# Conditioning every block in fp32 with row tiles of the array, in place of an fp16 high/low split

## The reference

```python
# x (128, 64, 512) fp32, itok (128,) in 1..198, weights (200, 64, 64), W1 (2048, 512), W2 (512, 2048)
w = weights[conditions]
c = jnp.einsum('bct,bcd->bdt', x, w)                 # conditioning, one 64x64 matrix per batch
h = gelu(einsum('bsd,hd->bsh', c, ternarize(W1)) + b1)
y = einsum('bsd,hd->bsh', h, ternarize(W2)) + b2
scale = jnp.max(jnp.abs(y)) / 7 + 1e-8               # over the whole tensor
out = x + jnp.clip(jnp.round(y / scale), -7, 7) * scale
```

## Time and profile before

| | |
|---|---|
| median of 3 runs | 1046.1 us |
| the profiled execution | 1043.87 us |
| its span, first to last instruction | 1042.1 us |
| mean granted TensorE clock | 0.966 of full |
| TensorE busy | 938.8 us (90%) |
| VectorE, ScalarE, GpSimd busy | 648.3, 553.5, 157.8 us |
| HBM read, written | 60.89, 16.78 MB |

### The profile page before, as it was taken

The page is one execution under the profiler, slowest core; times in us unless marked ns, Lnnn a source line. Parts: engine busy times, 40 slices in busy tenths (PEclk is TensorE's granted clock), DMA queues, the critical chain, the costliest instruction groups (busy, mean ns, idle before and its releaser), DMA issues.

```text
span 1042.1 us, 15005 instructions
## 1 busy us (share of the span) xinstructions
PE 938.8 (90%) x5265; PEld 449.3 (43%) x5265; DVE 648.3 (62%) x1005; ACT 553.5 (53%) x708; POOL 157.8 (15%) x213
## 2 busy tenths in 40 slices
PE   0599999999999999999999999999999999999600
PEld 0355444444444444444444444444444444444200
DVE  3499766666665657666666666566666656633492
ACT  3389282736446473828274564738282645536290
POOL 4022303030110303030301102030303021000000
PEclk9799999999999999999999999999999999999855
DMA  6610030211121211203011112112030111104899
GB/s 219 201 44 4 18 74 12 63 26 42 44 47 40 50 40 36 54 10 73 17 40 45 45 40 50 40 45 46 10 79 11 40 46 44 40 0 173 297 395 384
DMA packets 40560, 77.89 MB, mean 75 GB/s; under 512 B 3920, under 2 KB 4320, under 8 KB 40032
## 3 DMA queue, kind: packets, MB, share of 16 engines
q1 hardware_dynamic: 36272, 73.47, 24.1%
q0 software_dynamic: 4096, 3.94, 1.3%
q10 hardware_dynamic: 176, 0.27, 0.1%
HBM read 60.89 MB, written 16.78 MB: 75 GB/s over the span
## 4 chain that ended last, share of the span: by engine, by line
PE 77%; issue 10%; ACT 4%; DVE 3%; POOL 2%; DMA 1%; DVEq 0%; ACTq 0%; SPq 0%; POOLq 0%
PE ps L430 38%; PE ps L442 35%; PE ps L418 3%; ACT y L667 2%; PE ps L460 1%; ACT y L639 1%; POOL ws L342 1%; DVE st L684 1%; DMA yx<-in_x 1%; DVE y L797 0%; DVE y L932 0%; DVE wts L794 0%; DMA condb<-in_itok_B 0%; DVE st L743 0%; POOL wg L342 0%
## 5 line engine op out<-in xcount | busy, mean ns | idle before, releaser
L430 PE MATMUL ps<-yc,wts 128*128 128x512 f16 x2048 | 447.3, 379 | 0.2 <-ACT g L571 0.2
L442 PE MATMUL ps<-wts 128*128 128x512 f16 x1920 | 419.3, 379 | 0.7 <-ACT wts L595 0.7
L430 PEld LDWEIGHTS ps<-yc,wts 128*128 128x128 f16 x2048 | 199.5, 98 | 238.5 <-ACT g L571 0.7
L442 PEld LDWEIGHTS ps<-wts 128*128 128x128 f16 x1920 | 185.8, 98 | 220.4 <-ACT wts L595 0.9
L717 DVE SCALAR_TENSOR_TENSOR wts<-g,st,wts 128x512 f16<-128x512 f32 x256 | 186.4, 749 | 144.4 <-ACT wts L576 142.5
L571 ACT ACTIVATE g<-ps,b1t,st 128x512 f32<-128x512 f32 x256 | 197.9, 773 | 117.8 <-PE ps L430 107.2
L576 ACT ACTIVATE wts<-g,st 128x512 f16<-128x512 f32 x256 | 181.0, 713 | 0.0
L558 ACT ACTIVATE xs<-yx,st 128x2048 f16<-128x2048 f32 x28 | 56.1, 2002 | 143.5 <-DVE st L752 143.5
L364 POOL PARTITION_ALL_REDUCE st<-st x46 | 21.5, 468 | 670.2 <-DVE st L686 414.7
L342 POOL DMA_INDIRECT wg<-in_L_cond_weights,ids x112 | 106.5, 951 | 41.3 <-issue 29.6
L722 DVE SCALAR_TENSOR_TENSOR y<-ps,st,b2b 128x512 f32 (+1 forms) x56 | 41.8, 747 | 78.1 <-PE ps L442 78.0
(11 more groups left out here) (118 smaller groups left out, 379.4 us busy)
## 6 DMA issues: line engine op xcount, KB each, us to landing
yx<-in_x SPq DMA_DIRECT2D x56, 512.0 KB, 6.1
wts<-in_x SPq DMA_DIRECT2D x5, 1024.0 KB, 5.5
y<-in_x SPq DMA_DIRECT2D x5, 1024.0 KB, 10.4
out<-wts SPq DMA_DIRECT2D x10, 512.0 KB, 10.6
y<-in_L_ffn_W SPq DMA_DIRECT2D x8, 512.0 KB, 8.8
y<-in_L_ffn_W SPq DMA_DIRECT2D x4, 1024.0 KB, 8.3
wts<-in_x SPq DMA_DIRECT2D x8, 512.0 KB, 7.3
out<-y SPq DMA_DIRECT2D x4, 1024.0 KB, 12.6
```

What stands on the lines that cost most here:

```text
L430: last = nc.tensor.matmul(psH[:, j % HB, :], T1T[:, k, j * P:(j + 1) * P], csp[:, a, k, :], start=(k == 0 and a == 0), stop=(k == KT - 1 a ...
L442: last = nc.tensor.matmul(psY[:, r % 2, :], hsp[:, a, j, r * P:(r + 1) * P], T2T[:, j, :], start=(j == 0 and a == 0), stop=(j == HT - 1 an ...
```

## The change

All 16 blocks are conditioned in fp32 by one code. `xd` becomes a buffer of its own, loaded once for a block by four transfers: partitions 0 to 63 (s = 0) hold two batches of each half (h), partitions 64 to 127 (s = 1) the other two. `wg` shrinks to four matrices side by side in each side's 64 partitions, gathered by four indirect DMAs with 128 indices. Each matmul takes 64 partitions, either side alone, and writes that side's bank of `psC`. The splitting of x and w, its scales, its reductions and its semaphores are gone on VectorE, ScalarE and GpSimd, and so is `cinv` in the copy of c. `idt`, a temporary of the index arithmetic, moves to a part of y, and block 0's x of the tail goes to `xd`.

```diff
 # SP
-            load_direct(0)
-            sp.wait_ge(w_gathered[1], 16 * HALF)
+            def load_x(first_batch):
+                for s in range(2):
+                    for h in range(2):
+                        sp.dma_start(xd[s * C:(s + 1) * C, 2 * h:2 * h + 2, :],
+                                     x_cbt[:, bass.ds(first_batch + HALF * h + 2 * s, 2), :]).then_inc(xd_loaded, 16)
+            load_x(0)
+            sp.wait_ge(w_gathered, 16 * RT)
             for n in range(RT):
                 sp.dma_start(w2s[:, n, :], W2_v[:, n, :]).then_inc(w2_loaded[n], 16)
-            load_half(0, DIRECT * BB)
-            sp.wait_ge(t1_made, WCH)
-            sp.wait_ge(w1abs_made, LOADS)
-            load_direct(1)
-            with sp.Fori(1, 2 * (NB - DIRECT)) as n:
-                sp.wait_ge(x_split, n)
-                load_half(n, n * HALF + DIRECT * BB)
+            with sp.Fori(1, NB) as b:
+                sp.wait_ge(c_made, 2 * b)
+                load_x(b * BB)
 # GpSimd
-            def gather(b, columns, direct=False):
-                nc.gpsimd.tensor_copy(ids[:, :], columns).then_inc(ids_made, 1)
-                pool.wait_ge(ids_made, b + 1)
+            def gather(b, columns):
+                by_side = columns.rearrange("p (h s j) -> p s h j", h=2, s=2)
+                for s in range(2):
+                    side = slice(s * C, (s + 1) * C)
+                    nc.gpsimd.tensor_copy(ids[side, :].rearrange("p (h j) -> p h j", h=2), by_side[side, s, :, :])\
+                        .then_inc(ids_made, 1)
+                pool.wait_ge(ids_made, 2 * b + 2)
                 pool.sem_inc(pool_waited, 1)
-                for j in range(BB):
+                for r in range(RT):
...
             all_max(max2_part, 1, mx2r, mx2, max2_all)
+            pool.wait_ge(max2_all, 1)
             pool.wait_ge(c_made, 2)
-            gather(1, idx[:, BB:2 * BB], direct=True)
+            gather(1, idx[:, BB:2 * BB])
...
                 all_max_c(i + 1)
+                pool.wait_ge(cmax_all, i + 2)
                 gather(i + 2, columns)
-                for h in range(2):
-                    all_max(xw_part, 2 * i + 1 + h, xwr, xw, xw_all)
 # TensorE
+            def condition(b, half):
+                pe.wait_ge(xd_loaded, 64 * b + 64)
+                pe.wait_ge(w_gathered, 16 * RT * (b + 1))
+                pe.wait_ge(c_copied, 2 * b + half)
+                tiles(half, psC)
+            def tiles(half, bank):
                 for k in range(KT):
-                    tk = slice(k * P, (k + 1) * P)
-                    if direct:
...
-                    for j in range(HALF):
-                        n = half * HALF + j
-                        for a in range(2):
-                            last = nc.tensor.matmul(psC[:, k, j * C:(j + 1) * C], xs[:, n, tk], ws[:, a, n, :],
-                                                    start=(a == 0), stop=(a == 1))
+                    for j in range(2):
+                        for s in range(2):
+                            side = slice(s * C, (s + 1) * C)
+                            last = nc.tensor.matmul(bank[:, s, k, j * C:(j + 1) * C],
+                                                    xd[side, 2 * half + j, k * P:(k + 1) * P], wg[side, 2 * half + j, :],
+                                                    start=True, stop=True)
                 last.then_inc(c_made, 1)
 # ScalarE: high_x is gone from block_step and hidden; copy_c copies without a scale
 # VectorE, block_step
                 max_y(i, 1, tile_y(1), slot(1))
-                if not last_block:
-                    max_xw(2 * i, 0, i + 2)
                 store_y(i, 2, tile_y(2))
                 max_y(i, 2, tile_y(2), slot(2))
-                if not last_block:
-                    scale_xw(2 * i, 0, lk)
-                    low_x(2 * i, 0)
...
                 for j in range(HT):
                     low_h(i + 1, j)
-                    if j == 1:
-                        max_xw(2 * i + 1, 1, i + 2)
-                    if j == 3:
-                        scale_xw(2 * i + 1, 1, lk)
-                    if j == 6:
-                        low_x(2 * i + 1, 1)
```

More of the change, by code:

```diff
@@ L157, in build @@
         parts = rest.rearrange("p (w m n t) -> p w m n t", w=3, m=4, n=2)
-        xtail = [place(xs[:, :, :].rearrange("p b t -> p (b t)").bitcast(FP32)),
+        xtail = [place(xd[:, :, :].rearrange("p r t -> p (r t)")),
                  t1_rows[:, 0, :, :, :], t1_rows[:, 1, :, :, :],
@@ L183, in build @@
         sum2, sum2r = stat(2), stat(2)
-        xw, xwr, bxw, pxw, rxw, sxw = (stat(2) for _ in range(6))
-        cinv = stat(2)
         n2c, alpha2 = stat(), stat()
@@ L333, in _ @@
             link(nc.gpsimd.tensor_tensor(idx[:, :], idx[:, :], idt, ALU.add))
-            def gather(b, columns, direct=False):
-                nc.gpsimd.tensor_copy(ids[:, :], columns).then_inc(ids_made, 1)
-                pool.wait_ge(ids_made, b + 1)
+            def gather(b, columns):
[5 more added lines that the diff above has]
+                pool.wait_ge(ids_made, 2 * b + 2)
                 pool.sem_inc(pool_waited, 1)
-                for j in range(BB):
-                    side = slice(j % 2 * C, (j % 2 + 1) * C)
+                for r in range(RT):
                     nc.gpsimd.indirect_dma_start(
[L343 to L348, removed]
+                        out=wg[:, r, :], out_offset=None, in_=w_rows[:, :],
+                        in_offset=bass.IndirectOffsetOnAxis(ap=ids[:, r:r + 1], axis=0)).then_inc(w_gathered, 16)
+            gather(0, idx[:, 0:BB])
             nc.gpsimd.memset(ident[:, :], 0.0)
@@ L476, in _ @@
             nc.tensor.transpose(psY[:, 0, 0:HT], b1r[:, :], idf[:, :]).then_inc(b1_turned, 1)
-            condition(0, 0, direct=True)
-            condition(0, 1, direct=True)
+            pe.wait_ge(xd_loaded, 64)
+            pe.wait_ge(w_gathered, 16 * RT)
+            tiles(0, psC)
+            tiles(1, psC0)
             pe.wait_ge(b1_ready, 1)
@@ L545, in _, with copy_c @@
             act.dma_start(b2b[:, :], b2.rearrange("(a n) -> a n", a=1).to_broadcast([P, T])).then_inc(b2_loaded, 16)
-            def copy_c(b, half, direct=False):
+            def copy_c(b, half, bank=psC):
                 act.wait_ge(c_made, 2 * b + half + 1)
                 rows = slice(half * HALF * C, (half + 1) * HALF * C)
[L550 to L557, removed]
-                nc.scalar.activation(xs[:, js, :], xd, ACT.Copy, scale=sxw[:, 0:1])
-                nc.scalar.activation(ws[:, 0, js, :], wg[:, js, :], ACT.Copy, scale=sxw[:, 1:2]).then_inc(xhi_made, 1)
+                nc.scalar.activation(cf[:, :, rows].rearrange("p k (s r) -> p s k r", s=2), bank, ACT.Copy).then_inc(c_copied, 1)
             def high_c(b):
@@ L613, in _ @@
             relu1(1)
-            copy_c(0, 0, direct=True)
-            copy_c(0, 1, direct=True)
+            copy_c(0, 0)
+            copy_c(0, 1, psC0)
             relu1(2)
@@ L640, in _, with block_step @@
                     .then_inc(w2_counted, 1)
-            def block_step(i, first_block=False, last=False):
+            def block_step(i, first_block=False):
                 if not first_block:
@@ L646, in block_step @@
                     copy_c(i + 1, 0)
-                copy_c(i + 1, 1, direct=first_block)
+                copy_c(i + 1, 1)
                 high_c(i + 1)
-                if not last:
-                    high_x(2 * i, 0)
-                hidden(i + 1, lambda j: high_x(2 * i + 1, 1) if j == 5 and not last else None)
+                hidden(i + 1, lambda j: None)
             block_step(0, first_block=True)
-            with act.Fori(1, NB - 2) as i:
+            with act.Fori(1, NB - 1) as i:
                 block_step(i)
-            block_step(NB - 2, last=True)
             act.wait_ge(y_stored, RT * (NB - 1))
```

89 lines of the change are left out of this document (14 added, 75 removed).

## The result

| | before | after |
|---|---|---|
| median of the runs | 1045.0 us (4 runs) | 1071.4 us (4 runs, 1070.7 to 1072.1) |
| the profiled execution | 1043.87 | 1072.14 |
| its span | 1042.1 | 1070.3 |
| HBM read | 60.89 MB | 44.38 MB |

The kernel got slower: the ratio is 1.0253, 95% interval 1.0237 to 1.0269, that is +26.4 us between the medians and +28.3 between the profiled executions. 1075 was forecast, in a range of 1052 to 1122.

The account below looks back on a forecast made before the run. TensorE was taken to bound the blocks, behind a start chained through GpSimd. Terms +33.3 + 0.7 - 4.5 - 0.2 = +29.3 us on a 1046.1 median gave 1075.4, stated as 1075; range 1052 to 1122 us.

Parts of the forecast that it names:

- The bound: Blocks from 153 to 953 us: the chain of waits never leaves TensorE, so conditioning time there is kernel time.
- The halves of blocks 2 to 15: 28 conditioning halves on TensorE: each 2.12 us, 1.19 more than now, +33.3 us in all.
- the crossing: TensorE going over to row tiles and back around each half: 0.33 us, at most 0.62, at least nothing.
- 94 to 112 ns for a load: Time an fp32 load occupies its rows in conditioning; 16 per row tile make 1.50 to 1.79 us a half.
- two tails of 163 ns: Matmul tails on changing to row tiles and back: 2 x 163 = 0.33 us a half, loads perhaps still running ahead.
- Block 1: Its two halves, already fp32, keep 1.79 us for loads and pay only the change of tiling: +0.7 us.
- The start: GpSimd's chain before the blocks: four gathers in place of eight, 9.7 us becoming 5.2, thus -4.5 us.
- a possible 4.8 us: Extra gain if less traffic in front shortened the 10.54 us stretch before the first reduction to 5.76; not counted.
- Block 0's 0.2 us: TensorE's idle time in block 0 for the held-up gelu, removed by relieving VectorE and ScalarE: -0.2 us, else nothing.
- serialized loads: Rival in conditioning: the two tiles' loads don't run side by side, a half 3.58 + 0.33 us; +83, 1129 us; chance 0.16.
- partly bare loads: Rival in conditioning: loads overlap only across tiles, a half 2.69 + 0.33 us; +56, 1102 us; chance 0.14.
- free loads: Rival in conditioning: loads half as long or fully hidden, a half 0.90 us; -7, 1039 us; chance 0.10.

Follow-up runs that it names:

- doubling: Changed kernel with the 16 conditioning matmuls of each half in blocks 1 to 15 run twice in a row: 1125.4 us, +53.2.
- the first experiment: Changed kernel with each half's matmuls reordered, all of partitions 0 to 63 first, then 64 to 127: 1124.4 us.
- the equal 1033.2: Kernel before with block 0 in row tiles, four gathers, most constants after the first reduction, and W2's loads held until that reduction: 1033.2 us (1033.4 without the wait).

## Why the prediction was right

**The bound** was read rightly: TensorE has no idle time from block 2 to the end of its work, before and after, and putting VectorE's work back moved no block. One reading was loose: the chain of waits leaves TensorE at 904.7 and not at 953, and counts the 73.5 us from 909 on as GpSimd's "issue"; that TensorE works on until 980.65 stands in its own rows.

**The halves of blocks 2 to 15.** Forecast 2.12 us each, +33.3; measured 2.03, +30.8. The parts: loads 1.79 forecast, 1.79 measured by doubling; the crossing 0.33 forecast, 0.24 measured. That row tiles load side by side was the choice that mattered, and the order of the sides shows it: 2.03 us a half with the tiles in turn, 3.42 with one after the other. The choice of 94 to 112 ns for a load by its record was sound: a load of half the columns has a record 53 ns shorter and a step of 58 ns for 112. The Trainium skill's rule that a load's time goes by its columns (TensorE: Matmul & The Clock Gate, LDWEIGHTS) agrees with 188 ns at 64 rows, 192 at 128, and 135 at half the columns.

The crossing was right in kind, but its two tails of 163 ns were a guess with a wrong reason, that loads may still run ahead: they do not (159.72 against 159.65 above), and the whole still comes to less, 0.24 us for there and back, with none between fp16 and fp32. The Trainium skill's rule that a change of tiling mode drains TensorE (TensorEngine Tiling (Array Packing), Key Properties) agrees with that gap in the loads.

**Block 1.** Forecast +0.7. Its second half pays the 0.24 us; the half at 86.7 us lies where ScalarE's stores are waited for anyway. So +0.2 on the path.

**The start.** Forecast -4.5, measured -4.3, by luck in part: the gathers gave 4.4 as forecast, and two stretches that I had let stand moved and nearly cancelled: GpSimd began 1.3 us later, and the one ahead of the reduction was 1.1 us shorter. In other kernels with the same start the reduction stood up to 2.2 us earlier and 1.3 us later. I had named the traffic of W2 as a possible 4.8 us in the 10.54 and not used it; it is real (5.3 us when held back). In the changed kernel W2's loads (from 23.78) still begin ahead of that stretch (25.49), so it kept nearly all of it.

**Block 0's 0.2 us** went as forecast: TensorE's line L403 has 0.0 us of idle time where the earlier trace rows had 0.21.

**The sum** was 29.3 against 28.3 between the profiled executions, with the halves 2.5 us and block 1 0.5 too dear, and 1.7 us of scatter in the tail, which was forecast as nothing, that covers part of it. Of the rivals, serialized loads is what the first experiment looks like, near its price (3.42 us a half with the crossing, forecast 3.91). The partly bare loads (3.02 us a half) are excluded by the measured 2.03 and the steps of 112 ns, the free loads by the same steps and by the kernel with half the loaded columns.

## What to carry to other kernels

For small fp32 matmuls, count the columns loaded, not the columns streamed: here 16 loads on each tile, 112 ns apart, set a half's 1.79 us, and twice the moving columns added 0.06. Row tiles load side by side only as long as neighbours in the queue alternate between them, and each visit to them cost 0.24 us. A split into fp16 parts that looks wasteful (32 matmuls, three engines at work on the parts) is half as dear on TensorE (0.93 us a half against 1.78 in fp32 without tiles), and where TensorE is the bound that is what counts. Look at the start as a chain of its own: four gathers fewer and the constants behind the first reduction made the kernel before 10.5 us faster (1043.9 to 1033.4, ratio 0.9895), some 4 of it because GpSimd's stretch then began ahead of W2's traffic. It is the fastest of all that ran here but for the equal 1033.2.

## What the runs showed of the hardware that I had not expected

- The stretch ahead of GpSimd's first partition_all_reduce takes 5.56 to 5.72 us where W2's transfers begin behind it or in its second half (mean DMA share 0.00 to 0.52), and 8.67 to 10.93 where it begins behind theirs (0.88 to 1.02).
- The granted clock halved for some 3 us behind 3.32 us of fp32 work on one row tile after the other, in five products with TensorE busy throughout (and in block 1's behind a wait). In the changed kernel, with 1.93 us of both tiles at once, no product of the loop's blocks was longer than 20.83 or 7.01 us. What in the work makes the difference was not tried.
- No weight load runs ahead over a change between the whole array and row tiles: the load queue stands idle for 0.42 us ahead of a half, and 0.07 us behind it.
- A matmul's record can hold another's time: 272 ns for 64 fp32 columns stayed 272 with 128 columns and became 218 when only the loads were shortened.
